# Dequantisation scales split on 128 partitions, with a reordered start and a deferred down product

## The reference, cut to what matters

```python
x = x + 0.5 * ffn(layernorm(x))
x = x + attn(layernorm(x))
x = x + 0.5 * ffn(layernorm(x))
# ffn: h = silu(x @ Wg) * (x @ Wu);  out = h @ Wd
# W[k, n] = scales[g_idx[k], n] * (w4[k, n] - (z4[g_idx[k], n] + 1))
```

## Time and profile before

| | before |
|---|---|
| median of 3 runs | 838.71 us (838.26 to 839.10) |
| profiled execution, its own time | 838.12 us |
| its span in the trace | 836.3 us |
| PE busy | 817.5 us, 98% of the span |
| DVE, ACT, POOL busy | 498.5, 274.4, 250.7 us |
| granted TensorE clock, mean | 0.999 |

### The profile page before, as it was taken

The page is one execution under the profiler, slowest core; times in us unless marked ns, Lnnn a source line. Parts: engine busy times, 40 slices in busy tenths (PEclk is TensorE's granted clock), DMA queues, the critical chain, the costliest instruction groups (busy, mean ns, idle before and its releaser), DMA issues.

```text
span 836.3 us, 10580 instructions
## 1 busy us (share of the span) xinstructions
PE 817.5 (98%) x3944; PEld 672.6 (80%) x3944; DVE 498.5 (60%) x815; ACT 274.4 (33%) x471; POOL 250.7 (30%) x200
## 2 busy tenths in 40 slices
PE   5899999999999999999999999999999999999998
PEld 5677778878888888788888887888878888888786
DVE  8999956755754543556866885545346734443452
ACT  3333342455211211332665872121123311111221
POOL 5555624552204260203055362061411201110100
PEclk9999999999999999999999999999999999999999
DMA  5898848966555343144043159634445064444121
GB/s 157 266 338 283 296 143 293 362 262 246 212 216 174 129 154 88 63 152 151 1 165 138 39 177 336 241 127 165 138 131 174 25 215 157 146 144 157 29 102 50
DMA packets 72721, 143.04 MB, mean 171 GB/s; under 512 B 25374, under 2 KB 36320, under 8 KB 67678
## 3 DMA queue, kind: packets, MB, share of 16 engines
q1 hardware_dynamic: 65116, 131.15, 45.7%
q10 hardware_dynamic: 6690, 6.98, 2.4%
q0 software_dynamic: 864, 4.23, 1.9%
HBM read 104.36 MB, written 37.98 MB: 170 GB/s over the span
## 4 chain that ended last, share of the span: by engine, by line
PE 88%; DVE 6%; issue 3%; SPq 1%; DMA 1%; POOL 1%; ACT 1%; DVEq 0%; POOLq 0%
PE ps L802 46%; PE ps L795 38%; PE ps L813 2%; DVE wi L1700 2%; PE ps L1191 2%; DVE qs L1794 1%; SPq L560 1%; DMA qs<-in_L_ffn_up_qweight 1%; DVE xn L1734 1%; DVE wf_d L1817 0%; POOL wd L2214 0%; POOL wp L2214 0%; DVE hT L1700 0%; DVE tab_first L505 0%; DVE wf L1820 0%
## 5 line engine op out<-in xcount | busy, mean ns | idle before, releaser
L795 PE MATMUL ps<-blk,ring 128*128 128x512 f32 (+1 forms) x1386 | 321.1, 390 | 0.1
L795 PEld LDWEIGHTS ps<-blk,ring 128*128 128x128 f32 (+1 forms) x1386 | 256.6, 185 | 58.4 <-DVE blk L1700 0.5
L802 PE MATMUL ps<-wd,hT 128*128 128x512 f32 (+1 forms) x1056 | 251.9, 391 | 3.6 <-POOL wd L2214 2.3
L802 PEld LDWEIGHTS ps<-wd,hT 128*128 128x128 f32 (+1 forms) x1056 | 196.9, 188 | 46.7 <-POOL wd L2214 3.7
L2266 POOL TENSOR_TENSOR h<-h,u 128x512 f32<-128x512 f32 (+1 forms) x33 | 42.7, 1294 | 321.9 <-ACT h L1439 321.9
L802 PE MATMUL ps<-xT,wp 128*128 128x512 f32 x480 | 112.6, 390 | 1.3 <-POOL wp L2214 0.9
L802 PEld LDWEIGHTS ps<-xT,wp 128*128 128x128 f32 x480 | 89.9, 188 | 20.6 <-POOL wp L2214 1.3
L1703 DVE TENSOR_TENSOR u<-ps,p1s 128x512 f32<-128x512 f32 (+1 forms) x66 | 45.3, 687 | 96.5 <-PE ps L795 96.5
L1439 ACT ACTIVATE h<-h 128x512 f32<-128x512 f32 (+1 forms) x33 | 20.9, 633 | 176.6 <-DVE h L1703 176.6
L1703 DVE TENSOR_TENSOR h<-ps,p1s 128x512 f32<-128x512 f32 (+1 forms) x33 | 22.8, 691 | 64.1 <-PE ps L795 64.1
L1703 DVE TENSOR_TENSOR u<-ps,u 128x512 f32<-128x512 f32 (+1 forms) x66 | 45.6, 691 | 25.6 <-PE ps L795 24.6
(11 more groups left out here) (129 smaller groups left out, 894.8 us busy)
## 6 DMA issues: line engine op xcount, KB each, us to landing
ring<-wsaved SPq DMA_DIRECT2D x29, 1024.0 KB, 5.1
ring<-wsaved SPq DMA_DIRECT2D x33, 768.0 KB, 4.3
wsaved<-wp SPq DMA_DIRECT2D x10, 1024.0 KB, 4.9
stream<-xres SPq DMA_DIRECT2D x32, 256.0 KB, 2.1
xn<-stream SPq DMA_DIRECT2D x8, 1024.0 KB, 7.6
xres<-stream SPq DMA_DIRECT2D x32, 256.0 KB, 3.4
wfull<-wf ACTq DMA_DIRECT2D x20, 256.0 KB
wsaved<-wp SPq DMA_DIRECT2D x10, 512.0 KB, 3.2
```

The costliest lines, as they stand in the source:

```text
L795: mm = pe.matmul(ps[0:w, bank, :], ring[:, slot, which, a, kt, 0:w], blk[:, which, b, kt, :], start=not onto and kt == 0 and n == 0, stop= ...
L802: mm = pe.matmul(bank_ap, lhs(a), rhs(b), start=first and n == 0, stop=last and n == 2)
```

## The change

It has four parts.

1. **Scales.** Only tiles 0 and 1 are still split on 76 partitions in the start (one `load_scales` for gate and one for up, POOL's `first_left_gu`, one `table_gu` on DVE). All columns are also loaded flat, 64 partitions of 86 columns for each of gate and up (`sc_flat`, 128 partitions together), and split by POOL in four steps (`scale_parts`); six DMAs issued by ACT bring the three parts of both to PE's rows (`tab_rest`). The steps in `plain_top` of DVE are gone.
2. **Down product.** In `plain_top` of PE row tile 3 of each down product comes after the next tile's gate product; row tiles 0 to 2 stay behind the up product, and none is left between gate and up of the same tile but that one.
3. **Start.** ACT issues x first. DVE does the statistics of x right after the zero points of gate and up, and the zero points of down after `unpack(0)`, now on 80 partitions of 8 words. SP issues `grp`, the load of down's zero points, the flat scales and down's index.
4. **SP's order.** Unit 1 is still issued behind the store of down's zero points, which now waits for the count that DVE reaches after them.

```diff
-TAB_TILES = ((0, 2), (2, 4), (4, 7), (7, NT))
-TAB_SPLIT = 7
+TAB_TILES = 2
...
+        SP_ROWS = 64
+        SP_COLS = GK * INTER // SP_ROWS
...
-        FIRST_STEPS, ZERO_STEPS = 4, PACK + 1
+        FIRST_STEPS, PART_STEPS = 3, 7
+        ZERO_STEPS, TAB_STEPS = PACK + 2, PACK + 3
+        FLAT_LOADS, PART_LOADS = 32, 128
...
+        def scale_parts(pool, step):
+            step(lambda: pool.tensor_copy(sc_part[0][:, :], upper(sc_flat[:, :])))
+            step(lambda: pool.tensor_tensor(out=sc_left[:, :], in0=sc_flat[:, :], in1=sc_part[0][:, :], op=ALU.subtract))
+            step(lambda: pool.tensor_copy(sc_part[1][:, :], upper(sc_left[:, :])))
+            step(lambda: pool.tensor_tensor(out=sc_part[2][:, :], in0=sc_left[:, :], in1=sc_part[1][:, :], op=ALU.subtract))
...
# SP, the start
+            sp.dma_start(grp[:, :], groups).then_inc(d_grp, 16)
+            sp.dma_start(zq_d, flat(zeros[2], ZC_D)).then_inc(d_zq_d, 16)
             sp.dma_start(idt[:, :], ident).then_inc(d_small, 16)
             sp.dma_start(shift[:, :], shifts).then_inc(d_small, 16)
-            sp.wait_ge(s_tab, 2 * ZERO_STEPS + 1)
+            for m in range(2):
+                sp.dma_start(sc_flat[SP_ROWS * m:SP_ROWS * (m + 1), :], flat(scales[m], SP_COLS)).then_inc(d_cut_rest, 16)
+            sp.wait_ge(s_tab, ZERO_STEPS)
             sp.wait_ge(s_cut, 1)
             for m, row in enumerate((Z_ROW, Z_UP)):
                 sp.dma_start(zb_gu[row:row + GK, :], zs_gu[m][m * ZP:(m + 1) * ZP, :]).then_inc(d_zb, 16)
+            sp.wait_ge(s_cst, 4)
...
+            sp.dma_start(idx_d[:, 0:NT - 1], ...)
+            sp.dma_start(idx_d[0:INTER - last, NT - 1:NT], ...)
             sp.dma_start(rows_d[:, 0:HID], scales[2]).then_inc(d_rows, 16)
-            sp.dma_start(rows_d[:, HID:D_ROW].bitcast(BF16), zb_d.rearrange("p c j -> p (c j)")).then_inc(d_rows, 16)
+            sp.wait_ge(s_tab, TAB_STEPS + PACK + 1)
+            sp.dma_start(rows_d[:, HID:D_ROW].bitcast(BF16), zb_d).then_inc(d_rows, 16)
             load_units(sp, [1])
-            sp.wait_ge(s_cut, 2)
-            for m in range(2):
-                load_scales(sp, m, REST_COLS, d_cut_rest)
             load_units(sp, [2])
...
# PE, scales_zeros and plain_top
-                for piece, (first, _) in enumerate(TAB_TILES):
-                    if i == first:
-                        pe.wait_ge(s_tab, tab_done(piece))
+                if i == 0:
+                    pe.wait_ge(s_tab, TAB_STEPS)
+                elif i == TAB_TILES:
+                    pe.wait_ge(d_cut_rest, PART_LOADS)
...
-                    if 1 < i < NT - 1:
-                        pe.wait_ge(s_wlo, made(2, i - 1))
-                        down(0, 0, i - 1, (0,))
+                    if i >= 2:
+                        down(0, 0, i - 2, (RT - 1,))
...
-                    if i == 1 or i == NT - 1:
+                    if i:
                         pe.wait_ge(s_wlo, made(2, i - 1))
-                        down(0, 0, i - 1)
-                    elif i:
-                        down(0, 0, i - 1, (1, 2, 3))
+                        down(0, 0, i - 1, range(RT if i == NT - 1 else RT - 1))
...
# ACT, the start
-            act.dma_start(zq_d, zeros[2]).then_inc(d_zq_d, 16)
+            for r in range(RT):
+                act.dma_start(xn0[:, 0, r, :], x[r * P:(r + 1) * P, :]).then_inc(d_x0[r], 16)
             act.wait_ge(s_cst, 1)
             for m in range(2):
-                load_scales(act, m, FIRST_COLS, d_cut_gu)
-            act.dma_start(grp[:, :], groups).then_inc(d_grp, 16)
-            for r in range(RT):
-                act.dma_start(xn0[:, 0, r, :], x[r * P:(r + 1) * P, :]).then_inc(d_x0[r], 16)
+                load_scales(act, m)
             load_units(act, [0])
...
             w_hi(1)
+            act.wait_ge(s_cut, PART_STEPS)
+            for m in range(2):
+                for n in range(3):
+                    row = FOLD * m + GK * n
+                    act.dma_start(tab_rest[row:row + GK, :], sc_part[n][SP_ROWS * m:SP_ROWS * (m + 1), :]).then_inc(d_cut_rest, 16)
             plain_top()
...
# DVE, plain_top and the start
-                    if i in (2, 4):
-                        left_gu_of(dve, tables, 1 + i // 2)
-                    if i in (3, 5):
-                        table_gu(dve, tables, 1 + i // 2)
...
-                    if i == 0:
-                        table_gu(dve, tables, 1)
...
-            dve.wait_ge(d_zq_d, 16)
-            unpack_zeros(dve, tables, zq_d, zi_d, (zb_d.rearrange("p c j -> p (c j)"), 1.0, 1.0))
             dve.wait_ge(d_zq_gu, 32)
             unpack_zeros(dve, tables, zq_gu, zi_gu, (zs_gu[0], 1.0, Z_LOW), (zs_gu[1], 1.0 + Z_BIAS, 1.0))
-            dve.wait_ge(d_idx_gu, 32)
-            clamp(dve, hots, GU_COLS, GK, S_ROWS)
-            dve.wait_ge(d_grp, 16)
-            compare_low(dve, hots, GU_COLS, 0, oh_gu[S_ROWS, :], S_ROWS)
-            one_hot(dve, hots, GU_COLS, 0, oh_gu[S_ROWS, :], S_ROWS)
             ln_stats(0, (0, 1))
             ln_var(0, (0, 1))
             ln_stats(0, (2, 3))
             ln_shift(0, (0, 1))
             ln_var(0, (2, 3))
+            dve.wait_ge(d_idx_gu, 32)
+            clamp(dve, hots, GU_COLS, GK, S_ROWS)
+            ln_shift(0, (2, 3))
+            dve.wait_ge(d_grp, 16)
+            compare_low(dve, hots, GU_COLS, 0, oh_gu[S_ROWS, :], S_ROWS)
+            one_hot(dve, hots, GU_COLS, 0, oh_gu[S_ROWS, :], S_ROWS)
             dve.wait_ge(s_cut, FIRST_STEPS)
-            table_gu(dve, tables, 0)
+            table_gu(dve, tables)
             dve.wait_ge(d_small, 32)
             unpack(0)
-            ln_shift(0, (2, 3))
+            dve.wait_ge(d_zq_d, 16)
+            unpack_zeros(dve, tables, zq_d, zi_d, (zb_d, 1.0, 1.0))
             dequantise(0)
             dequantise(1, unpack_next=False)
             rows_lo(0)
             unpack(2)
-            dve.wait_ge(d_cut_rest, 32)
-            left_gu_of(dve, tables, 1)
             plain_top()
...
# POOL, the start
-            cutter(lambda: pool.memset(sc_gu[S_ROWS, REST_COLS], 0.0))
             pool.wait_ge(s_cst, 8)
             pool.wait_ge(d_cut_gu, 32)
             first_left_gu(pool, cutter)
+            indices = maker(pool, s_idx)
             deviation(0, 0, 2)
+            pool.wait_ge(d_cut_rest, FLAT_LOADS)
+            scale_parts(pool, cutter)
             deviation(0, 2, RT)
-            indices = maker(pool, s_idx)
             pool.wait_ge(d_idx_d, 32)
```

More of the change, by code:

```diff
@@ L184, in scratch @@
             return over_wp(name, shape, dtype)
-        TAB_COLS = (NT - TAB_SPLIT) * P
+        SP_ROWS = 64
+        SP_COLS = GK * INTER // SP_ROWS
+        sc_flat = scratch("sc_flat", [P, SP_COLS], F32)
+        sc_left = scratch("sc_left", [P, SP_COLS], F32)
+        sc_part = [scratch(f"sc_part{n}", [P, SP_COLS], BF16) for n in range(3)]
         Z_ROWS, Z_UP = slice(Z_ROW, Z_ROW + 3 * GK), Z_ROW + 2 * GK
         S_ROWS = slice(0, FOLD + 3 * GK)
-        sc_gu = scratch("sc_gu", [P, INTER], F32)
-        left_gu = scratch("left_gu", [P, TAB_COLS], F32)
+        sc_gu = scratch("sc_gu", [P, TAB_TILES * P], F32)
+        left_gu = scratch("left_gu", [P, TAB_TILES * P], F32)
         ZP = 16
@@ L480, in unpack_zeros, with table_gu @@
                    for zb, add, by in results))
-        def scale_cols(piece):
-            first, end = TAB_TILES[piece][0] * P, min(TAB_TILES[piece][1] * P, INTER)
-            return sc_gu[S_ROWS, first:end], left_gu[S_ROWS, 0:end - first], tab_gu(S_ROWS, first, end)
         def tab_gu(rows, first, end):
-            if first < TAB_SPLIT * P:
-                return tab_first[rows, first:end]
-            return tab_last[rows, first - TAB_SPLIT * P:end - TAB_SPLIT * P]
+            if first < TAB_TILES * P:
+                return upper(tab_first[rows, first:end])
+            return tab_rest[rows, first:end]
         def first_left_gu(pool, step):
-            s, left, _ = scale_cols(0)
+            s, left = sc_gu[S_ROWS, :], left_gu[S_ROWS, :]
             step(lambda: pool.tensor_scalar(left, upper(s), keep[S_ROWS, 0:1], None, ALU.mult))
             step(lambda: pool.tensor_tensor(out=left, in0=left, in1=s, op=ALU.subtract))
-        def left_gu_of(eng, step, piece):
-            s, left, _ = scale_cols(piece)
-            step(lambda: eng.scalar_tensor_tensor(out=left, in0=upper(s), scalar=keep[S_ROWS, 0:1], in1=s,
+        def table_gu(eng, step):
+            left = left_gu[S_ROWS, :]
+            step(lambda: eng.scalar_tensor_tensor(out=tab_first[S_ROWS, :], in0=upper(left), scalar=keep[S_ROWS, 1:2], in1=left,
                                                   op0=ALU.mult, op1=ALU.subtract))
-        def table_gu(eng, step, piece):
-            _, left, dst = scale_cols(piece)
-            step(lambda: eng.scalar_tensor_tensor(out=dst, in0=upper(left), scalar=keep[S_ROWS, 1:2], in1=left,
-                                                  op0=ALU.mult, op1=ALU.subtract))
+        def scale_parts(pool, step):
```

(3 more changed lines are left out.)

34 lines of the change are left out of this document (16 added, 18 removed).

## The result

The changed kernel takes 841.3 us (median of 6 runs, 840.87 to 843.14) where the kernel before took 838.49 (6 runs): a ratio of 1.0037, with a 95% interval of 1.0024 to 1.005. It is slower by 2.8 us. (The ratio and its interval compare the single runs of the two kernels, so they need not equal the quotient of the medians.) The forecast was 840.0, no change on its slower side; the range of 837.0 to 843.2 holds the result. The interval lies just beyond the 0.2% that counts as no change, on the side that had the largest chance, 0.45.

What follows compares the result with a forecast made beforehand. PE was taken to bound the kernel, busy 817.5 of 836.3 us, with DVE making early weights just in time. A start loss of 5.4 less a loop gain of 4.15 gave +1.25, so 840.0 us; range 837.0 to 843.2.

Steps and rivals of the forecast that it cites:

- the side that had the largest chance, 0.45: Whole kernel: slower by over 0.2%, above 840.4 us; chance 0.45, against 0.38 within and 0.17 faster.
- the +1.25 us of the sum: Whole kernel: the start's loss of 5.4 us minus the loop's gain of 4.15 us.
- the signs named beforehand: Start and loop: unit 1 issued at 15 to 16, first product at 22 to 24, PE busy over 96% to 100 us.
- SP issues unit 1 late, the first product 5.4 us late.: Start: unit 1 waits behind down's zero points, so the first product starts at 23.0 instead of 17.56; bounds 2.9 and 8.3.
- The gain of the loop, 4.15 us.: Loop up to 100 us: removed PE waits worth 4.55, less 0.4 for ACT's issues; bounds 2.3 and 5.56 us.
- ACT's six issues cost 0.4.: Loop, tile 0: six `tab_rest` issues on ACT delay `silu` and gate 1's high half; 0.4 us, from nothing to 1.5.
- The clock as a rival, 0.15.: Start: PE idles, so the first 24 products run partly at half speed; +1.7 us, 841.7; chance 0.15.
- the fourth rival: Loop: transfers, not DVE, set the pace, so only 2.3 us is gained; +3.1, 841.8; chance 0.10.
- The rule on leading dimensions.: Scale loads: an outermost dimension under 16 confines a DMA to that many engines; flat loads could let unit 3 land sooner.
- The rival that the start is hardly late: Start: scales land early and `scale_parts` costs 1.1, so the first product starts near 21; -1.8 us, 836.9; chance 0.15.

Runs made afterwards that it cites:

- down_new_alone: The kernel before with only the down product moved to its new place; 837.27 us, ratio 0.9998 to the kernel before.
- start_old_down_old: The changed kernel with the start of the kernel before and the down product in its old place; 833.35 us, ratio 0.9944 to the kernel before.
- start_old: The changed kernel with the start of the kernel before, but down's zero points still on 80 partitions; 832.08 us, ratio 0.9935 to the kernel before.
- warm_long: The changed kernel with 18 more warm-up products between the transposes and the scales of tile 1; 844.42 us, ratio 1.0084 to the kernel before.
- after_again: The changed kernel unedited, measured again in a later set; 841.55 us, ratio 1.0044 to the kernel before.
- parts_behind: The changed kernel with POOL's flat split of the scales moved behind the second inverse deviation; 840.53 us, ratio 1.0027 to the kernel before.
- down_old: The changed kernel with the down product in its old place; 842.78 us, ratio 1.0067 to the kernel before.
- pool_order: The changed kernel with units 1 to 3 issued after gate and up's zero points, and POOL's deviations each ahead of a split; 838.4 us, ratio 1.0007.
- unit1_early: The changed kernel with unit 1 issued right after the zero points of gate and up are stored; 838.12 us, ratio 1.0022 to the kernel before.
- unit1_and_pool: The changed kernel with only unit 1 issued after gate and up's zero points, and POOL's deviations each ahead of a split; 837.02 us, ratio 0.9995.
- kept_warm: The changed kernel with six more warm-up products between the transposes and the scales of tile 1; 841.53 us, ratio 1.0054 to the kernel before.

## Why the prediction was right, and where it was not

The sign and most of the way were right: SP's order delays unit 1, DVE stands on it, and the loop gives part back. The time lies in the range, but the change came out at more than twice the +1.25 us of the sum. In the spans it is +2.90: the start lost 1.08 us more than forecast and the slow clock 1.56, while the loop gave back 0.99 more. That these errors partly cancelled was luck.

Of the signs named beforehand, DVE's wait on the deviation and on unit 1 and PE's busy share came (0.89 us missed from 24.04 to 100 us, so 98.8%). Unit 1's issue at 16.72 and the first product at 24.04 lie just outside their ranges, and one wait on `hs`, 0.89 us, stayed. Step by step:


- **SP issues unit 1 late, the first product 5.4 us late.** Right; measured 6.48. Unit 1's last issue was at 18.70 (predicted 17.7), it landed in 2.63 (2.5), the first product was at 24.04 (23.0). The mis-sized term is the landing of the scales behind x: they were there at 7.47 (4.05 + 3.42), not at 6.4. POOL's chain carried this to DVE, which stood until 12.56 (11.7). `scale_parts` itself took 10.18 to 11.76, 1.6 us, as read from the rows (1.75).
- **The gain of the loop, 4.15 us.** It measured 5.14 (4.33 + 0.81), inside the bounds. But its division failed: I gave 3.35 us to the deferred down product (1.05 and 2.3) and 1.20 to the table. down_new_alone and start_old_down_old show that the first is nothing measurable, and the second, priced at 1.20, is the gain: with nearly nothing else changed, start_old_down_old is 4.9 us below the kernel before. I had the evidence, DVE busy for 77.55 of 82.44 us, and still read the waits on `wd` as a matter of place.
- **ACT's six issues cost 0.4.** The working does not give this number: six issues of 4.6 us against 1.93 us of idling leave 2.7, and the step from there to 0.4 is not shown. They took 23.71 to 27.54, 0.64 each instead of 0.77, and `silu` of tile 0 came after them without delay: PE's late and slower first products hid them. In start_old, where these ran at full clock, PE waited 0.58 us for `tab_rest` itself at tile 2, which no term had.
- **The clock as a rival, 0.15.** It came: 7.29 instead of 5.73. The price of 1.7 us on the total was not borne out, since warm_long took the slow clock away and gained nothing. The granted clock was 0.50 to 0.54 in each microsecond from 24 to 27, after 3.2 us of idling: the lower of the two levels. By the Trainium skill, TensorE: Matmul & The Clock Gate (Part 1), an idle engine is at 1.2 GHz; the trace agrees.
- **What the sum did not have: a transfer holds the loop once DVE is faster.** Only the fourth rival named it, with a chance of 0.10, and I used "DVE waited for a DMA once" against it. Its price did not come, since the loop gained 5.14 us and not 2.3, but its mechanism did. In the changed kernel, in after_again and in start_old the `down` unit of tile 3 takes 8.5, 10.4 and 8.9 us to land and holds `hs`. It fixes gate 4 in these and swallows changes of about 1.5 us ahead of it; in parts_behind, down_old and pool_order PE does not wait there.
- **The rule on leading dimensions.** Unit 3 no longer had the broadcast of the scales ahead of it, and in unit1_early DVE still waited for it: its last issue at 21.76 took 4.79 us to land, and 4.75 in warm_long, against 5.27 in the kernel before and 5.91 in down_new_alone, where the broadcast was ahead of it. So most of that landing is not the broadcast's. Whether the difference of 0.5 to 1.2 us is, stays open, since the traffic differs too.
- **The rival that the start is hardly late** needed its waits gone; they were there. unit1_and_pool shows that even then the gain is lost to the later units.

## What to carry to other kernels

When a step is moved later, follow each in-order queue behind it to the end: here one wait on SP held not one unit but all of them, and repairing the first moved the wait to the third. Credit a removed wait to what made its source late, not to the place where it shows. Compare variants at a fixed piece of work, as gate 4 here, and first make sure that the same products lie on either side of it; here three changed sides in some kernels. Where the variants then need nearly the same time from there on, the difference lies ahead of the cut, and one sees that a later wait swallows what an earlier stage gains. Profile a variant more than once before reading less than 2 us from it: one kernel's gate 4 differed by 2.2 us.

## What the runs showed of the hardware that I had not expected

- The lower clock can come back after less than 3 us of idling: in warm_long 2.97 us in the middle of dense products put the next 12 at a granted clock of 0.67 (4.33 instead of 2.98 us); in kept_warm 2.67 us ahead of the first ones were enough. In after_again 2.44 us left it at 1.00 (12 products in 3.00 us), as did gaps of up to 1.2 us after 17.56 in the kernel before.
- The down unit of tile 3, one DMA of 256 KB, took 8.5 to 10.4 us to land when the DMA engines were busy throughout (a DMA share of 0.99 from 47 to 52 us and 1.12 from 52 to 56 in the changed kernel). The last of the four 64 KB DMAs of unit 1 took 2.63 in a quieter stretch (a share of 0.57 while it was under way).
